# A graph network with an attention branch on one core: the branch's per-tile work moved into the rounds of the three edge stages

## The reference, cut to what matters

```python
xn = _layernorm(x)
# branch 1: three GAT layers over the edges (gather xh[src], softmax per dst, scatter-sum)
# branch 2, on the same xn (8 heads of 32):
q, k, v = split(xn @ Wqkv.T); q = elu(q) + 1; k = elu(k) + 1
kv = einsum('nshd,nshm->nhmd', k, v); ksum = k.sum(1)          # over ALL nodes
t = einsum('nlhd,nhmd,nlh->nlhm', q, kv, 1/(q . ksum + 1e-6))
x1 = layer_norm(t + xn, ln1_g, ln1_b)
mix = layer_norm(gelu(x1 @ W1.T + b1) @ W2.T + b2 + x1, ln2_g, ln2_b)
x = x + gnn(xn, edges) + mix
x = x + ffn(_layernorm(x))                                      # 8 experts, top 2
```

## Time and the profile before

| | us |
|---|---|
| median of 3 runs | 8544.74 (8540.32 to 8545.97) |
| the profiled execution's own time | 8543.02 |
| its span (first to last instruction) | 8541.2 |
| stretch from the first transfer of the mixing branch to the first of `node_phase` 0 | 597.71 |
| edge stage 0, first index copy to the next stage's start | 2137.61 |
| mean granted TensorE clock | 0.755 of full |

### The profile page before, as it was taken

One profiled execution on the slowest core, in us unless ns is written; L12 is line 12 of the kernel. 1 busy time (PEld: TensorE's weight loads), 2 busy tenths in 40 slices (PEclk: granted clock), 3 DMA queues, 4 the chain that ended last, 5 costly groups with the idle time before them and its releaser, 6 DMA issues. The chain is left out here.

```text
span 8541.2 us, 126708 instructions
## 1 busy us (share of the span) xinstructions
PE 4989.8 (58%) x21039; PEld 3648.4 (43%) x21040; DVE 5705.6 (67%) x15256; ACT 1375.1 (16%) x5317; POOL 5309.6 (62%) x5685
## 2 busy tenths in 40 slices
PE   1853566666666555666666665546666666652597
PEld 0652344444444433444444444334444444442355
DVE  3565667767676676677676766857676767678443
ACT  0322111111111031111111110311111111103333
POOL 1113777777777537777777775377777777752332
PEclk6986777777777757777777777577777777775799
DMA  2004555555555434444444443444444444436333
GB/s 72 0 3 139 159 160 160 162 158 164 158 164 158 114 106 139 133 136 133 133 135 133 136 133 98 128 137 136 133 137 133 137 133 137 133 103 208 77 55 77
DMA packets 518321, 1079.25 MB, mean 126 GB/s; under 512 B 131852, under 2 KB 310188, under 8 KB 517696
## 3 DMA queue, kind: packets, MB, share of 16 engines
q0 software_dynamic: 274368, 731.65, 32.0%
q1 hardware_dynamic: 242352, 342.64, 12.6%
q10 hardware_dynamic: 1152, 1.05, 0.0%
HBM read 941.45 MB, written 142.21 MB: 127 GB/s over the span
## 5 line engine op out<-in xcount | busy, mean ns | idle before, releaser
L963 POOL DMA_INDIRECT edges_G<-rows,edges_index x4980 | 4760.4, 956 | 1546.8 <-issue 1495.4
L1071 PE MATMUL edges_ps_o<-edges_G,edges_OH 128*128 128x264 f32 x9960 | 3474.5, 519 | 399.5 <-DVE acc L1253 380.8
L1071 PEld LDWEIGHTS edges_ps_o<-edges_G,edges_OH 128*128 128x128 f32 x9960 | 2522.7, 263 | 1145.3 <-DVE acc L1253 532.9
L1235 DVE TENSOR_TENSOR edges_G<-edges_G,edges_ps_w 128x1024 f32<-128x1024 f32 x1245 | 1501.4, 1206 | 0.0
L1253 DVE TENSOR_TENSOR acc<-acc,edges_ps_o 128x264 f32 x2490 | 1052.0, 422 | 275.9 <-DVE acc L1253 168.4
L1134 DVE TENSOR_TENSOR edges_tu<-edges_ad,edges_G 128x80 f32<-128x80 f32 x249 | 74.8, 300 | 1406.6 <-DMA edges_G<-rows,edges_index 1406.6
L1227 DVE TENSOR_TENSOR edges_OH<-edges_ps_iota,relT 128x512 f32<-128x512 f32 x1245 | 847.0, 681 | 1.8
L1046 PE MATMUL edges_ps_s<-ident,edges_greatest 128*128 128x128 f32 x249 | 115.5, 464 | 1121.3 <-DVE edges_greatest L1195 1088.9
L990 ACT ACTIVATE edges_ps_w<-edges_diff 128x80 f32<-128x80 f32 x249 | 60.0, 241 | 4167.7 <-DVE edges_diff L1215 4167.7
L1038 PE MATMUL edges_ps_s<-ident,edges_alpha 128*128 128x128 f32 x249 | 93.3, 375 | 918.7 <-DVE edges_alpha L1139 918.7
L1046 PEld LDWEIGHTS edges_ps_s<-ident,edges_greatest 128*128 128x128 f32 x249 | 44.5, 179 | 1222.5 <-DVE edges_greatest L1195 1187.2
(11 more groups left out here) (338 smaller groups left out, 5731.3 us busy)
## 6 DMA issues: line engine op xcount, KB each, us to landing
edges_rels<-rel SPq DMA_DIRECT2D x249, 640.0 KB
edges_G<-rows,edges_index POOLq DMA_INDIRECT x4980
xslot<-edges_blank SPq DMA_DIRECT2D x80, 650.0 KB
edges_links<-links SPq DMA_DIRECT2D x1992, 0.1 KB
rows<-node_ext POOLq DMA_DIRECT2D x147, 130.0 KB, 2.5
h<-node_Hn POOLq DMA_DIRECT2D x147, 128.0 KB, 2.5
edges_masks<-lanes SPq DMA_DIRECT2D x996, 15.0 KB
experts_X<-xslot SPq DMA_DIRECT2D x105, 130.0 KB, 2.1
```

The source lines that it names most:

```text
L963: g.indirect_dma_start(G[n][:, s, 0:RW], None, dr["rows"], bass.IndirectOffsetOnAxis(index[n][:, s:s + 1], 0)).then_inc(gathered[n], 16)
L1071: mm = pe.matmul(ps_o[g % BANKS][:, 0:GW], OH[:, 2 * g + j, :], G[n][:, 2 * g + j, :], start=(j == 0), stop=(j == 1))
L1235: v.tensor_tensor(g4[:, :, :, 0:D], g4[:, :, :, 0:D], ps_w[:, 4 * k:4 * k + 4, :].unsqueeze(3).broadcast_to([P, 4, H, D]), ALU.mult).then_ ...
```

## The change

The eleven stages of the mixing branch are gone but for one: `turn_weights` is now one stage that transposes all ten 128-row blocks of the three weights in a ring of four PSUM banks, and loads three 256-word vectors as columns. The rest runs tile by tile in the edge stages, one node tile a round, each tile several rounds behind the one before in its chain (so 49 to 56 of a stage's 83 rounds have mixing work, the others none):

- `node_phase` 0 stores its normalized tiles to a DRAM tensor `xn` instead of `h`.
- **Edge stage 0: keys.** SP loads tile t in round t; PE transposes it in round t+1 (`turn_x`), projects keys and values in t+2 (`project`: two matmuls of 512 columns), and multiplies in t+3 (`mix_in`: four matmuls of 130 columns; relu and exponential parts of the key feature are not added first, but multiplied one after the other); ACT copies and makes features (Copy, Relu, Copy, Relu, Exp); DVE adds the product to an SBUF sum (`sum_kv`, 260 columns, once a round) and at the stage's end copies 16 blocks to `KV`.
- **Edge stage 1: queries.** `turn_x`, `project` (four matmuls of 128 columns), `mix_in` (four of 132); DVE `read_out` (six operations: add 1e-6, reciprocal, multiply in PSUM, add to R, `bn_stats`, `bn_aggr`), `invert` (two small ones); ACT `deviation` (Sqrt) and `centre`; SP stores the tile to `x1` (normalized, without gain and offset).
- **Edge stage 2: the two layers.** ACT applies gain and offset while it copies (`copy_x`), Gelu, `take_sum`; PE `project`, and a `mix_in` of two matmuls of 256 columns, one of a single row for b2 and two of 128 columns that add x1 back; DVE `measure`, `invert`, and `gain` (two operations of 256 columns); SP stores to `mix`.
- To make room in PSUM, `BANKS` is 3 in edge stages 0 and 2, and 4 in stage 1 (a table `BANK_OF` says which group has which bank; group g waits for the `add` of the group before it in its bank), and `ps_iota` and `ps_w` share a bank, for which DVE waits for ACT's `weights_ready` before its first one-hots of a round.
- PE's mixing work stands after `sums` 9 and **before `turn_back`**. DVE's is spread between its own steps (`next(extra)`), with the late part ahead of and behind the last one-hots. ACT's `centre` opens its round, the rest closes it. SP's two DMAs close its round. POOL gets nothing.

```diff
-    BANKS = 5
+    BANKS = 4 if layer == 1 else 3
+    BANK_OF = (0, 1, 2, 3, 0, 1, 2, 3, 1, 2) if layer == 1 else (0, 1, 2, 0, 1, 2, 0, 1, 2, 1)
...
         def over_windows(eng, step, ahead, early, mixes=True):
...
+            if mixes:
+                unrolled(-early, RING * FILLED)
+                looped(FILLED, FULL, True)
+                unrolled(RING * FULL, RING * DRAINED)
+                looped(DRAINED, rounds, False)
...
         # PE
-                    wait_past(pe, added, WG * w + g + 1 - BANKS)
+                    wait_past(pe, added, WG * w + g + 1 - since_bank(g))
...
+            def mixes(i, n):
+                t1, t2, t3 = (tile(i, n, k) for k in (1, 2, 3))
+                if t3 is not None:
+                    mix_in(t3, (n - 3) % XS)
+                if t2 is not None:
+                    project(t2, (n - 2) % XS)
+                if t1 is not None:
+                    count = t1 // XM if isinstance(t1, int) else RING // XM * i + (n - 1) // XM
+                    turn_x(t1, (n - 1) % XM, count + 1)
...
                 if here:
                     sums(i, n, range(9, 10))
+                if mix:
+                    mixes(i, n)
                 if exists(i, n, 2):
                     turn_back(*later(i, n, 2))
...
         # DVE
+                if one:
+                    v.wait_ge(weights_ready, 2 * (RING * i + n) + 3)
+                next(extra, None)
                 if here:
                     onehots(i, n, 4)
+                    next(extra, None)
                     b = next(blocks)
                     fade_sums(i, n, b)
+                    next(extra, None)
                     add(i, n, 0, b)
...
+            if layer == 0:
+                v.wait_ge(kv_added, NB)
+                for g in range(2):
+                    for h in range(GH):
+                        r = slice(h * M_D, (h + 1) * M_D)
+                        v.tensor_copy(st["KV"][r, g, r], kv[r, g, r]).then_inc(kv_out, 1)
+                        v.tensor_copy(st["KV"][r, g, P + h:P + h + 1], kv[r, g, P:P + 1]).then_inc(kv_out, 1)
...
-                turn_weights(nc, "turn_qkv", io["mix_Wqkv"], WT, st["ident"])
-                turn_weights(nc, "turn_w1", io["mix_W1"], W1T, st["ident"])
-                turn_weights(nc, "turn_w2", io["mix_W2"], W2T, st["ident"])
-                move_tiles(nc, "load_x", XN, io["x"])
-                normalize_tiles(nc, "norm_x", XN, None, None)
-                mix_keys(nc, st, XN, WT, KV)
-                mix_queries(nc, st, XN, WT, KV)
-                normalize_tiles(nc, "norm_mix1", XN, io["mix_ln1_g"], io["mix_ln1_b"])
-                mix_mlp(nc, st, io, XN, W1T, W2T)
-                normalize_tiles(nc, "norm_mix2", XN, io["mix_ln2_g"], io["mix_ln2_b"])
-                move_tiles(nc, "store_mix", dr["mix"], XN)
...
+                turn_weights(nc, st, io)
+                node_phase(nc, 0, st, io, dr)
+                for layer in range(3):
+                    edge_phase(nc, layer, st, io, dr)
+                    if layer < 2:
+                        node_phase(nc, layer + 1, st, io, dr)
```

More of the change, by code:

```diff
@@ L48 @@
 XW = C + 4
+M_HEADS = 8
+M_D = C // M_HEADS
+GH = P // M_D
+KW = P + GH
+VW = P + 2
+FILLED, FULL, DRAINED = 2, NB // 4, 14
 CLEARED = 5
@@ L890, in exists, with since_bank @@
             return not isinstance(i, int) or 0 <= RING * i + n + k < NW
+        def since_bank(g):
+            return next(d for d in range(1, WG + 1) if BANK_OF[(g - d) % WG] == BANK_OF[g])
         def blocks_of(eng, w):
@@ L951, in _, with step @@
                 sp.wait_ge(slots_cleared, 16 * CLEARING)
+            else:
+                for slot in range(2):
+                    sp.wait_ge(xh_out[slot], 16 * len(range(slot, NB, 2)))
         @block.gpsimd
         def _(g):
-            def step(i, n):
+            def step(i, n, mix):
                 w = RING * i + n
@@ new lines, in deviation, with centre @@
+            def deviation(t, slot):
+                a.wait_ge(moments, t + 1)
+                wait_past(a, mshift_ready, t - 1)
+                a.activation(msd[:, slot, :], mmv[:, slot, 1:2], ACT.Sqrt, bias=eps[:, :]).then_inc(msd_ready, 1)
+            def centre(t, slot, old):
+                a.wait_ge(mshift_ready, t + 1)
+                a.wait_ge(r_ready, t + 1)
+                if layer == 1:
+                    if not isinstance(old, int) or old > 0:
+                        a.wait_ge(xh_out[slot], 16 * old)
+                    to = xh[:, slot, :]
+                else:
+                    wait_past(a, done, t)
+                    to = ps_gain
+                a.activation(to, R[:, slot, :], ACT.Identity, bias=mshift[:, slot, :], scale=mscale[:, slot, :]).then_inc(xh_ready, 1)
@@ new lines, in gain, with early_mix @@
+            def gain(t, slot, old):
+                v.wait_ge(xh_ready, t + 1)
+                v.tensor_tensor(ps_gain, ps_gain, rows2[:, 0, :], ALU.mult).then_inc(gained, 1)
+                yield
+                v.wait_ge(gained, t + 1)
+                if not isinstance(old, int) or old > 0:
+                    v.wait_ge(xh_out[slot], 16 * old)
+                v.tensor_tensor(xh[:, slot, :], ps_gain, rows2[:, 1, :], ALU.add).then_inc(done, 1)
+                yield
+            def early_mix(i, n):
+                t4, t6 = tile(i, n, 4), tile(i, n, 6)
+                if layer == 0 and t4 is not None:
+                    yield from sum_kv(t4)
+                if layer == 1 and t4 is not None:
+                    yield from read_out(t4, n % 2, n)
+                if layer == 2 and t6 is not None:
+                    yield from gain(t6, n % 2, t6 // 2 if isinstance(t6, int) else 2 * i + (n - 6) // 2)
@@ L1431, in turn_weights @@
+def turn_weights(nc, st, io):
+    ident = st["ident"]
+    parts = [(io["mix_Wqkv"], st["WT"]), (io["mix_W1"], st["W1T"]), (io["mix_W2"], st["W2T"])]
+    ROWS = sum(w.shape[0] for w, _ in parts) // P
+    with Phase(nc, "turn") as ph:
+        w = ph.sb("w", [P, ROWS, C])
+        ps = [ph.ps(f"ps{k}", [P, 512]) for k in range(4)]
         w_in = ph.sem("w_in")
+        small_in = ph.sem("small_in")
         turned = ph.sem("turned")
@@ L1451, in _ @@
         def _(v):
-            for r in range(rows // P):
-                v.wait_ge(turned, r + 1)
-                v.tensor_copy(out[:, :, r * P:(r + 1) * P], ps[r % 2][:, 0:C].rearrange("p (k o) -> p k o", k=2)
-                              ).then_inc(copied, 1)
-            v.wait_ge(copied, rows // P)
-def tile_of(t, b):
-    return t[:, bass.ds(b, 1), :].rearrange("p a c -> p (a c)")
-def stage_tiles(g, buf, stage, staged, turned):
-    def step(i, half, last):
-        b = 2 * i + half
-        g.wait_ge(turned, b + 1)
-        g.tensor_copy(stage[:, half, :], tile_of(buf, b)).then_inc(staged, 1)
-    over_tiles(g, step)
```

763 lines of the change are left out of this document (309 added, 454 removed).

## The result

The changed kernel takes 7934.98 us (median of 4 runs, 7932.3 to 7940.17), the kernel before 8543.78 us in the same session: a ratio of 0.9289, 95% interval 0.9272 to 0.9305, so 7.1% less. The forecast was 7966 us with a range from 7950. The time lies 31 us under the forecast and 15 us under the range. The profiled execution took 7940.17 us, its span is 7937.8, its mean clock 0.777. The profiled executions alone differ by 25 us from the sum of the prediction (7965.1 against 7940.2); the other 6 us are the step from the profiled execution to the median, where the forecast went up by 1 us and the measurement down by 5.

A forecast was written before the change was run, and what follows sets the result against it. POOL's gathers were taken to pace the edge stages (25.26 us a round), with the mixing branch alone on the path: 8543.0 - 597.7 + 13.8 + 3.0 + 3 = 7965.1, forecast as 7966 us, range 7950 to 8050.

The forecast's parts named there:

- The stretch removed: Mixing branch ahead of `node_phase` 0, between two barriers with nothing hidden in it: 597.7 us saved.
- the one `turn_weights`: Single weight-turning stage ahead of `node_phase` 0: 13.8 us added, bounds 9.5 and 20.3.
- The copies to `KV`: 16 copies after the last `add` of stage 0, wholly on the path: 3.0 us added.
- some 4: Sign of being right: DVE's wait for gathers in stage 0's mixing rounds falls from 5.6 to some 4 us.
- 25 us in hand: Edge stages: once per stage DVE and PE can fall about 25 us behind before POOL stops.
- the one on ACT, SP and POOL: Edge rounds: ACT's and SP's additions are covered, POOL gets nothing; cost zero.
- the section on the port rule: Edge rounds: a gather stretched 0.22 us during DVE's bf16 compare; new SBUF-to-SBUF `mshift` could do the same.
- rival B: New DVE work stretches POOL's gathers in stages 1 and 2: +22 us, 7988 us; three a round +65; chance 0.08.
- the likeliest case: The forecast of 7966 us holds, own range 7955 to 7995; chance 0.79.
- Three drains with fewer banks: Last window of each edge stage, PE's sums with fewer banks: 1 us each, 3 us in all, bounds 0 and 20.
- Rival A: Edge stages: PE stays at 1.2 GHz and becomes the bound: +253 us, 8219 us; it or a part, chance 0.10.
- Rival C: Edge rounds: `turn_back` behind mixing work makes DVE and PE take turns: +836 us, 8802 us; chance 0.02.

The follow-up runs named there:

- before_banks3: Kernel before with three PSUM banks for the sums in place of five, nothing else: 8543.43 us, ratio 1.0002.
- the larger dose: Changed kernel with projection matmuls issued 4 times over in stage 0, 6 times in stages 1 and 2, ahead of `turn_back`: 7965.19 us, ratio 0.9324.
- the other place: Changed kernel with the same repeated projection matmuls, but PE's mixing work behind `turn_back`: 7936.77 us, ratio 0.9292.
- after_bad_b: Changed kernel with 5, 3 and 4 DVE copies (0.2 us each) ahead of the compares in mixing rounds of stages 0, 1, 2: 7968.05 us, ratio 0.9314.
- after_good: Changed kernel, two DVE copies ahead of the compares in rounds without mixing, one in stage 0's mixing rounds, on the 10,023 us chip: ratio 0.9417.

## Why the prediction was off, by its own steps

**What held.** The stretch removed less the one `turn_weights` was -583.9, and measured -584.7 (12.2 us for the turning, where 13.8 stood, and a start 0.7 us later). POOL paced all three stages. Nothing added to DVE or PE in the rounds cost time by its length. The copies to `KV` took 2.1 us where 3.0 stood. DVE's wait for gathers in rounds with mixing was 4.6 to 4.8, 4.0 to 4.2 and 3.5 us in stages 0, 1 and 2 where "some 4" and "2 to 3" were expected: the additions were right in kind and some were sized too large. The "25 us in hand" showed itself in the run with more PE work.

**The step that failed** is the one on ACT, SP and POOL, "POOL gets nothing: zero". It took POOL's round of 25.26 us as a constant, though the section on the port rule had found a stretch of 0.22 us inside the round that it looked at. That section asked whether new DVE work could add stretches (rival B, +22 to +65 us). It didn't ask whether new DVE work could move the compare that already made them. It did: beside the compares of the 17th to the 49th window (33 rounds with mixing) there are 0.19, 0.24 and 0.08 us of stretches in all in stages 0, 1 and 2, where the kernel before has 7.1, 8.1 and 4.6. Over all windows the stretches beside compares fell by 36 us, those beside other operations rose by 6, and the three strings measured -31.4 us. It has the opposite sign of rival B and no term in the sum, and since the likeliest case's range also began at 7955, nothing reached down to 7935. The most that the term could be was in the trace: 18.7 + 19.7 + 12.8 = 51 us of stretches, which would have put the range's low end near 7915.

Not all of it is the mixing operations' doing: 10 of the 36 us come from rounds that have none. There the compare starts 4.72 to 4.81 us after the sum of the scores, where the kernel before has 4.59 to 4.68. A round of each shows the cause, the new wait for `weights_ready` ahead of the first one-hots (0.29 us after `leak`'s start, 0.16 before):

```profile
4818.47 0.24 DVE L1139 SCALAR_TENSOR_TENSOR edges_alpha<-edges_tu 128x80 f32<-128x80 f32 x1
4818.63 0.69 DVE L1227 TENSOR_TENSOR edges_OH<-edges_ps_iota,relT 128x512 f32<-128x512 f32 x1
...
4822.69 1.00 DVE L1121 TENSOR_SCALAR edges_OHT<-edges_rels,lane 128x1280 bf16<-128x1280 bf16 x2
```

```profile
4216.27 0.24 DVE L1423 SCALAR_TENSOR_TENSOR edges_alpha<-edges_tu 128x80 f32<-128x80 f32 x1
4216.56 0.69 DVE L1511 TENSOR_TENSOR edges_OH<-edges_ps_c,relT 128x512 f32<-128x512 f32 x1
...
4220.65 1.01 DVE L1405 TENSOR_SCALAR edges_OHT<-edges_rels,lane 128x1280 bf16<-128x1280 bf16 x2
```

This 0.13 us moves the compares of those rounds out of the last row of the table: 60 of 75 stand there before, 12 after, and the other 63 in the first two rows. No run has the wait alone.

**Terms too small or too large.** Three drains with fewer banks, 3 us: 0 in the time of `before_banks3`, though its traces have each stage's last `add` 0.4 to 0.5 us later. The edges of the stages took 12.8 us more (1.8 + 5.2 + 1.2 + 4.6) where 6.0 stood. 2.1 of it are the `KV` copies, 1.7 the last window of stage 0 (45.8 us from the last gather to the last `add`, 44.1 before). From the last gather to the end the kernels of this study with no mixing in stage 2 vary from 918.6 to 923.4 us and those with it from 920.3 to 926.7 (the chip of the long times left out), so a part of the 4.6 is no effect of the change. The rest is open. A slip without bearing: the terms of the likeliest case add up to 7993 at the top, not 7995.

**Rival A**, PE staying at half its clock: no. The granted clock rose, from 0.77 to 0.82 to 0.84 with mixing, and to 0.90 to 0.97 with 6 us of PE work more a round. The Trainium skill (TensorE: Matmul & The Clock Gate, "A second HAM failure mode: psum-queue depth-cycling") describes short idle gaps of PE between groups that cycle through banks, at which the clock goes back and forth and throughput is lost; here three banks alone gave a mean clock of 0.744, where five had 0.755, and no loss of time.

**Rival B**: in sum the stretches fell and did not rise, but its mechanism is there in small, in the 4.6 us beside `fade_sums` in stage 2. The port rule behind it was sound in kind. The Trainium skill (SBUF — State Buffer, "SBUF: two separate sides") has whichever of the two starts first hold the pair for its whole instruction and the other wait. The traces agree in part: compares that start at 0.50 to 0.65 us of the cycle take 0.68 us and not 0.545, and those that start at 0.96 to 1.25 have the next gather longer by 0.22 us on the mean. But a compare that starts in the first 0.45 us of a gather is not longer at all, so here the gather does not hold it up for its whole length.

**Rival C** (`turn_back` behind the mixing work): its new wait of "a few us" was 0.28, 0 and 0.28 us a round. Its mechanism is real, as the larger dose and the other place show, but it begins to cost only with some 6 us more of PE work a round, and then in one stage of three.

**Shown and not shown.** That the place of the compare sets the stretches is shown by moving it both ways in the kernel before, and again in the changed one. That the mixing operations, and in the other rounds the wait for `weights_ready`, are what moved it in the changed kernel is read from the trace (4.6 to 4.7 us from the sum of the scores to the compare before; then 4.9, 5.4 and 5.2 with mixing, 4.7 to 4.8 without) and is borne out by `after_bad_b`, which moved it back in a part of the rounds and lost 19 of the 31 us. That the scan and `fade_sums` stretch gathers in the same part of the cycle is read from traces alone. Why a DVE operation lengthens a gather in that part only is not shown.

## What to carry to other kernels

When one engine paces the kernel, its time per item is a measurement with losses inside it, and not a constant: look for the spread within the group (here 0.95 us against 1.17), find what stands beside the long ones, and put the sum of these losses into the range as a gain that any shift of another engine's work may give or take. Work that is slotted into slack is free only as to its length; it also moves everything behind it. Here the pacing engine and the one that it releases keep nearly the same phase round after round, so a shift of 0.1 to 0.4 us is repeated in every round. The same shift moves every operation behind it, and one of them may land in the bad part, as `fade_sums` did.

## What the runs showed of the hardware that was not expected

- 0.4 us of idle copies a round made the kernel before 38.5 us shorter. Nothing was removed.
- A DVE operation need not be long to have a stretched gather beside it: a scan of 0.42 us, with its operands in SBUF, has one (by 0.13 us on the mean, 107 times), and `fade_sums` of 0.43 us (by 0.16, 29 times in stage 2), where they start 0.96 us or more into the cycle. The compare of 2 x 1.5 us with one operand in PSUM had none in 498 windows, nor did the 83 scans with an operand in PSUM (L1148 of the kernel before) that start in the same part.
- One chip ran the kernel before in 10,023 us. The traces from there have DVE waiting for what they call "remote" (97.2 us before L1542 between 3000 and 4000 us of `after_good`) and POOL blocked; the ratios of the variants there (0.942) don't carry over.
- A string of 1660 gathers without its stretches took 2074 us on one chip and 2078 on another: 2.4 ns a gather, 12 us of the whole, the size of what is compared here. Only kernels that shared a chip, or their ratios, can be set side by side at this level.
